# The first attention's output projection with 512 queries streamed in one matmul, and a transpose back

## The reference, cut to what matters

```python
Q = (q @ w_qs)...; K = (q @ w_ks)...; V = (q @ w_vs)...       # q = layernorm(x), per head
attn = einsum('bnqd,bnkd->bnqk', Q + rel_embed_bias, K)
attn_pos = relative_shift(einsum('bnqd,nkd->bnqk', Q + rel_pos_bias, rel_k))
a = softmax(attn + attn_pos)
out = einsum('bnqk,bnkd->bnqd', a, V)                          # joined over the heads
x = x + out @ w_out + b_out
```

## Time and profile before

| what | value |
|---|---|
| median of 3 runs | 2921.26 us (2916.53 to 2924.25) |
| the profiled execution's own time | 2921.59 us |
| its span, first to last instruction | 2919.9 us |
| mean granted TensorE clock | 0.952 of full speed |
| TensorE busy | 2631.4 us (90% of the span), 14496 matmuls |
| VectorE busy | 2041.6 us (70%) |
| ScalarE busy | 1656.7 us (57%) |
| GpSimd busy | 355.0 us (12%) |
| HBM traffic over the span | 108 GB/s |

### The profile page before, as it was taken

How to read it: one execution, slowest core, us unless ns; L and a number is a source line. 1 busy time by engine, 2 the same in 40 slices (tenths; PEclk the granted TensorE clock), 3 DMA queues, 4 the chain that set the end, 5 groups by cost and what they waited for, 6 DMA issues and landing times.

```text
span 2919.9 us, 45160 instructions
## 1 busy us (share of the span) xinstructions
PE 2631.4 (90%) x14496; PEld 2047.8 (70%) x14496; DVE 2041.6 (70%) x5231; ACT 1656.7 (57%) x3430; POOL 355.0 (12%) x782
## 2 busy tenths in 40 slices
PE   2899999999999999999997079988998989998998
PEld 1688788888888888888886067765555555554777
DVE  3576776767767677677664078869777776773887
ACT  2566666666666666666664044544666656565454
POOL 0000000000000000000000123321221221222344
PEclk9999999999999999999999589978999999999999
DMA  2655556566655566556663100000000000000000
GB/s 84 206 203 205 183 200 209 200 214 207 211 205 201 205 214 214 205 195 205 214 208 110 51 6 1 1 1 1 1 1 1 1 1 1 1 1 1 9 8 15
DMA packets 98467, 321.63 MB, mean 110 GB/s; under 512 B 11556, under 2 KB 25508, under 8 KB 98020
## 3 DMA queue, kind: packets, MB, share of 16 engines
q1 hardware_dynamic: 98234, 318.74, 31.9%
HBM read 158.53 MB, written 157.29 MB: 108 GB/s over the span
## 4 chain that ended last, share of the span: by engine, by line
PE 77%; DVE 11%; ACT 5%; SPq 3%; issue 3%; DMA 1%; POOL 0%; DVEq 0%; ACTq 0%; POOLq 0%
PE ps L238 7%; PE ps L240 7%; PE ps L239 7%; PE ps L608 7%; PE ps L583 5%; PE ps L582 5%; PE ps L721 4%; PE ps L759 4%; PE ps L621 4%; PE ps L623 4%; PE ps L622 4%; PE ps L653 4%; PE ps L741 4%; PE ps L654 4%; PE ps L655 4%
## 5 line engine op out<-in xcount | busy, mean ns | idle before, releaser
L874 ACT ACTIVATE a_Ph<-ps 128x512 fp32r<-128x512 f32 x512 | 305.9, 597 | 474.5 <-PE ps L608 474.4
L1177 DVE CUSTOM_DVE_ANT_0 a_sp<-ps,a_sp 128x1024 f32<-128x1024 f32 x256 | 313.3, 1224 | 184.8 <-PE ps L240 178.9
L952 ACT ACTIVATE r_P<-ps 128x512 f32<-128x512 f32 (+3 forms) x768 | 327.7, 491 | 187.5 <-PE ps L741 183.2
L1183 DVE TENSOR_TENSOR a_Pl<-ps,a_Ph 128x512 fp32r<-128x512 f32 x512 | 349.3, 682 | 10.1 <-ACT a_Ph L874 9.8
L582 PE MATMUL ps<-a_fa,a_ua 128*128 128x384 f32 (+2 forms) x960 | 327.2, 353 | 5.0 <-DMA a_ub<-a_ua 2.6
L903 ACT ACTIVATE r_y<-ps 128x256 f32<-128x256 f32 x512 | 194.4, 385 | 220.9 <-PE ps L655 215.0
L867 ACT ACTIVATE a_sp<-a_sp,a_nm 128x1024 f32<-128x1024 f32 x256 | 295.0, 1152 | 29.4 <-DVE a_nm L1177 29.3
L608 PE MATMUL ps<-ident,a_sp 128*128 128x128 f32 x2048 | 309.0, 273 | 0.0
L653 PE MATMUL ps<-r_Wh,p_xh 128*128 128x512 f32 x512 | 223.0, 436 | 92.1 <-DVE r_Wl L1212 44.6
L721 PE MATMUL ps<-r_K,r_Q 128*128 128x512 f32 (+3 forms) x768 | 281.9, 402 | 18.0 <-DVE r_mx L1339 12.6
L608 PEld LDWEIGHTS ps<-ident,a_sp 128*128 128x128 f32 x2048 | 250.7, 141 | 61.6 <-issue 0.4
(11 more groups left out here) (203 smaller groups left out, 5631.0 us busy)
## 6 DMA issues: line engine op xcount, KB each, us to landing
scr<-a_rt SPq DMA_DIRECT2D x256, 576.0 KB, 3.1
a_sp<-scr SPq DMA_DIRECT2D x256, 512.0 KB, 4.4
a_wc<-wsp SPq DMA_DIRECT2D x24, 512.0 KB, 5.5
wsp<-a_wc SPq DMA_DIRECT2D x8, 512.0 KB, 4.6
a_ub<-a_ua SPq DMA_DIRECT2D x64, 44.0 KB
x<-in_q SPq DMA_DIRECT2D x4, 512.0 KB, 15.9
wst<-in_w1t SPq DMA_DIRECT2D x8, 256.0 KB
out<-x SPq DMA_DIRECT2D x4, 512.0 KB, 3.2
```

Source lines behind the costliest of these rows:

```text
L952: e.activation(self.P[:, pt, off:512], ps[:, bank, off:512], ACT.Exp).then_inc(S["b_exp"], 1)
L1177: e.tensor_tensor_reduce(out=w, in0=ps[:, 2:4, :].rearrange("p a n -> p (a n)"), in1=w, scale=-1.0, scalar=3e38, op0=ALU.add, op1=ALU.min, ...
L1183: e.tensor_tensor(self.Pl[:, n % 3, :], ps[:, 4 + n % 2, :], self.Ph[:, n % 3, :].bitcast(F32), ALU.subtract).then_inc(S["p_lo"], 1)
```

## The change

`out` now has the product of Wv and Wo as the stationary operand and the 512 columns of `osh` and `osl` as the moving one: one `mm3` instead of four, with 512 columns each. The result has features on the partitions, so it is turned: ScalarE copies it to a new tile in SBUF, `osb` (`o_turn`), and a new unit `back`, with `kq == 1` too but after the step's last `pv` and ahead of the extras, has TensorE transpose it in four parts into the same bank 7. VectorE's unit with the reciprocals and the sum into x moves from `out` to `back`, and so past the step's second `tlow`. The bank is handed over twice: to `back` by `o_turn`, and to the next user by `x_add`, as before.

```diff
-"ln_t g_mm prod_mm u_mm ga_mm r_mm s_mm t_mm pv_mm out_mm "
+"ln_t g_mm prod_mm u_mm ga_mm r_mm s_mm t_mm pv_mm out_mm back_mm "
...
         if tlive:
             p += [("tlow", pq, jb), ("pv", pq, ja)]
+        if kq == 1 and 0 < pq <= NQ:
+            p.append(("back", pq - 1, 7))
         p += extra.get(s, [])
...
+            self.osb = sb("osb", [128, 512])
...
     def first_attention_done(self, e):
-        e.wait_ge(S["out_mm"], NQ)
+        e.wait_ge(S["back_mm"], NQ)
...
     # TensorE
                 e.wait_ge(S["o_lo"], qd + 1)
                 e.wait_ge(*free[bank])
+                mm3(e, ps[:, bank, :], self.wc[:, slot, 0, 384:512], self.wc[:, slot, 1, 384:512], self.osh[:, :],
+                    self.osl[:, :]).then_inc(S["out_mm"], 1)
+                free[bank] = S["o_turn"], qd + 1
+            elif u[0] == "back":
+                _, qd, bank = u
+                e.wait_ge(*free[bank])
                 for k in range(4):
                     cs = slice(128 * k, 128 * k + 128)
-                    i = mm3(e, ps[:, bank, cs], self.osh[:, cs], self.osl[:, cs], self.wc[:, slot, 0, 384:512],
-                            self.wc[:, slot, 1, 384:512])
-                i.then_inc(S["out_mm"], 1)
+                    i = e.transpose(ps[:, bank, cs], self.osb[:, cs], ident[:, :])
+                i.then_inc(S["back_mm"], 1)
                 free[bank] = S["x_add"], qd + 1
...
     # ScalarE
+            elif u[0] == "out":
+                _, qd, bank = u
+                e.wait_ge(S["out_mm"], qd + 1)
+                e.activation(self.osb[:, :], ps[:, bank, :], ACT.Copy).then_inc(S["o_turn"], 1)
...
     # VectorE
-            elif u[0] == "out":
+            elif u[0] == "back":
...
-                e.wait_ge(S["out_mm"], qd + 1)
+                e.wait_ge(S["back_mm"], qd + 1)
```

More of the change, by code:

```diff
@@ L42 @@
     "d_w d_tab d_tmask d_f0 d_low d_wg d_wgr d_bo d_bias d_wo d_bof d_wb d_wvb d_bq d_bvo d_out "
-    "ln_t g_mm prod_mm u_mm ga_mm r_mm s_mm t_mm pv_mm out_mm "
+    "ln_t g_mm prod_mm u_mm ga_mm r_mm s_mm t_mm pv_mm out_mm back_mm "
     "f_mm f_tr f_proj b_pmm b_vmm b_mmm b_nmt b_smm b_pvmm b_ot0 b_ot1 b_at b_omm "
     "ln_sd g_exp wg_hi ws_hi wc_hi tab_hi u_hi ga_hi xn_hi nat_hi "
-    "r_act p_exp p_hi o_hi f_sig f_thi w1_hi wo_hi b_whi b_vhi b_y b_yh b_keys b_exp b_os b_ahi "
+    "r_act p_exp p_hi o_hi o_turn f_sig f_thi w1_hi wo_hi b_whi b_vhi b_y b_yh b_keys b_exp b_os b_ahi "
     "dve_step ln_var ln_xn xn_lo nat_lo wg_diff wg_lo w_mixed ws_lo wc_lo tab_lo x_bias "
```

## The result

The changed kernel takes 2930.5 us (median of 15 runs, 2924.27 to 2935.2), the kernel before 2919.21 us (15 runs, 2915.65 to 2924.25). The ratio is 1.0037 with a 95% interval of 1.0029 to 1.0046: slower by 0.37%, about 11 us. Forecast were 2916 us, within 2906 to 2926. The time lies outside the range, and the sign is the other one.

A forecast was written before the change was run, and what follows sets the result against it. TensorE's issuing was taken to bound the first attention, so savings on other engines were worth nothing. 2921.6 - 10.9 (quads) + 4.6 (gates) + 0.8 (stage end) = 2916.1 us, range 2906 to 2926.

The forecast's parts named there:

- the regular quad: TensorE per quad: projection saves 0.58 us, transposes behind it 0.02, transposes back cost 0.43; together -0.17 us.
- both rules that spoke against the change: Skill page's matmul gap (26 us slower) and 275 ns per transpose (quad 0.50 us longer); the forecast rejected both.
- ScalarE and VectorE in a regular quad: ScalarE's 0.60 us copy hidden, done 0.7 us before `back`; VectorE's later sum fits by 0.2 us; cost zero.
- Per quad: ... and 64 x 0.17 = -10.9 us: Projection in the first attention: the 0.17 us saved per quad counted for all 64 quads, -10.9 us.
- the wait for `Pl` of the earlier trace: TensorE waiting for the softmax weights' low part, 15.9 us in 15 places; possible gain 0 to 4 us, none counted.
- 3 x 1.5 = +4.6 us: Three gate logits behind `back`: TensorE stands 1.5 us each until bank 7 is free; bounds 0 and 6 us.
- a slip lands on TensorE only in the next content scores, over 2 us later: VectorE's sum, 0.2 us before the next score reduction is due: a delay reaches TensorE only later; no cost counted.
- the end of the stage: Last projection, with nothing beside it: 2.4 to 2.8 us to the sum instead of 1.98; +0.8 us, bounds 0.4 and 1.5.
- The rivals: More kept (0.28), ScalarE's copy late (0.07), transposes cost their duration (0.03), slower float32r matmul (0.02), small matmuls free nothing (0.01).
- The late copy on ScalarE: Rival: ScalarE's copy behind the exponential makes `back` wait; drifting quads add 16 us, 2932 us; chance 0.07.

The follow-up runs named there:

- a_twice: `a_apart` with a second ScalarE copy of each projection ahead of the one TensorE waits for: 2928.66 us, ratio 1.0033.
- hybrid: Changed kernel with the old projection kept in 20 of 64 quads (mix, gates and beside, four layernorm, 61 and 63): 2908.89 us, ratio 0.9968.
- a_few: Changed kernel with 3 of the 24 tiny logit matmuls at each of the three gates: 2916.09 us, ratio 0.9985.
- b_few: Kernel before with 3 of the 24 tiny logit matmuls at each of the three gates: 2910.59 us, ratio 0.997.
- a_apart: Changed kernel with each sequence's eleven layernorm and gate units moved to steps without kq == 1: 2920.71 us, ratio 1.0003.
- a_mix: `a_apart` with the weight mixes of heads 2 to 7 one step later: 2913.07 us, ratio 0.9978.
- b_mix: Kernel before with layernorm and gate units off kq == 1 steps and weight mixes one step later: 2912.6 us, ratio 0.9975.
- after: The changed kernel itself, against the kernel before: 2930.5 us, ratio 1.0037.
- hybrid_moved: `hybrid` with layernorm and gate units off kq == 1 steps and weight mixes one step later: 2902.23 us, ratio 0.9948.

## Why the prediction was wrong, step by step

**Right: the regular quad.** Forecast -0.17 us; measured -0.20 us, from 22.63 to 22.71 before to 22.45 mostly. Each term holds: 0.69 us for three large matmuls (0.71), 0.35 us for the transposes (0.36), 0.09 us for the one behind them (0.07). The distance between starts was the measure to take, not the 0.27 us durations, and both rules that spoke against the change failed, as the forecast had weighed them: by either the regular quad would have become longer.

**Right: ScalarE and VectorE in a regular quad.** The copy was covered with 0.7 us to spare, and `a_twice` shows it; the sum into x fitted with 0.22 us to spare.

**Wrong: "Per quad: ... and 64 x 0.17 = -10.9 us".** The factor 64 was the error. The argument rests on TensorE as the only bound, read from a stretch without side work, 600 to 800 us. In the five quads with a mix the wait for `Pl` of the earlier trace rows binds (9.8 of its 15.9 us lie there), and there a shorter projection is worth nothing while the transposes cost their whole 0.4 us and more. The forecast took that row as evidence that such waits are small (15.9 us), and even as a chance to gain; it should have asked in which quads they lie and priced those apart. Nor was it the largest wait for a working engine: the same window has 20.0 us in two places for `wsl`, both before the first quad. Size: 3.7 us lost where 5 x 0.17 us was to be won, or about 1 us per quad against the regular one. `hybrid`, with the old projection there, has the old distances.

**Wrong in size: "3 x 1.5 = +4.6 us" at the gates.** The wait itself was forecast well (1.5 us; 1.6 at the first gate by starts, 1.4 by the wait's own row). All three gates together cost 15.9 us more than before: 4.1 us of this wait; 6.8 us of clock (6.9, 6.8 and 3.4 us at the lower level against one stretch of 3.4 us, counting half of each); 5.1 us in the quads ahead of the logits, 1.7 us longer each (25.36 against 23.69), where layernorm's scaling stands behind the sum on VectorE and the copy behind the table load on ScalarE; 0.5 us in the quads behind; less 0.6 us of regular gain in the quads of the logits. The forecast had the first alone; the clock and VectorE's queue were put at nothing, without a word. The 9.7 us of `a_few` against `b_few` show the part without the clock. The clock's part is read from one pair of profiles and agrees with the 6 us from the times, but no run ties it to the wait. `a_apart` shows that the gates cost 1.8 us when the side units lie elsewhere. That "a slip lands on TensorE only in the next content scores, over 2 us later" was true of the sum alone and overlooked what was queued behind it.

**Right in place, smaller in size: the end of the stage.** 1603.85 - 1601.43 = 2.42 us from the projection's start to the sum, against 1.98: +0.4 instead of +0.8 us.

**The rivals.** None of them was this one. The late copy on ScalarE was real in seven places and 2.1 us (137 to 1550 us); the rest of the loss had not been put in words.

**What stays open.** The waits and the mixes are shown by removal. For the half clock, removal shows only that it needs the block of tiny matmuls at the gates; why it fell longer in the changed kernel is not shown. The pair `a_mix` and `b_mix` still stands at +0.5 us where 42 regular distances gain 0.2 us each. Half-clock stretches are a little more frequent in the changed versions in the early quads too (between 130 and 400 us: three in `after`, three in `a_apart`, four in `a_mix`, against three, two and two in their controls), which one profile of each cannot establish.

## What to carry to other kernels

A saving on a full engine holds only in the periods where that engine is the bound: tabulate every period of the loop, find those in which another engine is late, and price the change there separately, with its costs in full and its gain at zero. When a buffer or a bank is held longer, list every unit in the order that uses it or that is queued behind the moved instruction, the rare ones first. A form that wins in most periods and loses in few can be chosen per period: that was worth 0.3% here (`hybrid` against the kernel before, `hybrid_moved` against `b_mix`), where the same form everywhere cost 0.4%.

## What the hardware showed unexpectedly

TensorE's granted clock fell to the lower level (1.2 GHz) while the engine went on issuing. Ahead of each fall at a gate were matmuls of 8 columns, each with a load of 128 columns of its own, 0.11 us apart. With 24 of them it fell at 15 of 27 gates without any wait in front, and at three of three with 1.4 us of wait; with 3 of them and the same wait at none. It stayed down for 3.4 to 6.9 us, at the first gate of the changed kernel across six matmuls of 512 columns and the transposes and score matmuls behind them, issued without a gap. Falls elsewhere in this stage have no such block: in the kernel before, from 130 us on, they stand in three quads with a mix (260.4 to 263.8, 311.6 to 315.0, 366.2 to 369.6), close to a wait of 1.4 to 2.9 us for `Pl`.

Four fp32 transposes cost 0.35 us by their starts, a third of their summed durations, but the matmul behind a group of them takes 0.07 to 0.09 us longer than its like until the next one starts, in the trace of before and of after.
